# Softplus ahead of the residual and the logits, the first expert table in the last token tile, results ahead of ids, and own buffers for the last two results

## What is computed

```python
xs, z = split(x @ W_in.T)                       # 512 + 512
xc = silu(causal_conv_4_taps(xs) + conv_b)
a  = softplus((xc @ W_x.T)[:, :32] @ W_dt.T + b_dt)
x1 = layernorm(2 * x + (xc * a * silu(z)) @ W_out.T)
scores = sigmoid(x1 @ gate_w.T)                  # 16 experts in 4 groups of 4
# keep the 2 groups with the best sum of their 2 best (scores + bias); of these the top 4
# experts; weights = scores / their sum * 2.5
y = sum over the 4 experts of weight * (silu(x1 @ Wg) * (x1 @ Wu)) @ Wd   # inner size 128
y += (silu(x1 @ Ws_g.T) * (x1 @ Ws_u.T)) @ Ws_d.T                          # shared, 256
out = layernorm(2 * x1 + ... )                   # layernorm(x1 + (x1 + y))
```

## Time and profile before

| | |
|---|---|
| median of three runs | 603.64 us |
| profiled execution | 605.58 us, its span 603.8 us, mean granted TensorE clock 0.954 |
| TensorE busy / weight loads | 533.4 us (88%) / 449.9 us |
| VectorE | 434.6 us (72%) |
| ScalarE | 376.2 us (62%) |
| GpSimd | 335.4 us (56%) |
| chain that ended last | TensorE 55%, VectorE 24%, issue 7%, DMA 5% |

### The profile page before, as it was taken

How to read it: one execution, slowest core, us unless ns; L and a number is a source line. 1 busy time by engine, 2 the same in 40 slices (tenths; PEclk the granted TensorE clock), 3 DMA queues, 4 the chain that set the end, 5 groups by cost and what they waited for, 6 DMA issues and landing times.

```text
span 603.8 us, 11596 instructions
## 1 busy us (share of the span) xinstructions
PE 533.4 (88%) x3064; PEld 449.9 (75%) x3064; DVE 434.6 (72%) x1101; ACT 376.2 (62%) x960; POOL 335.4 (56%) x368
## 2 busy tenths in 40 slices
PE   2868899898998989979978899999999989998593
PEld 2557585676866768658666798999999979987582
DVE  3869689989899898997886567435344468787575
ACT  3675857757485574844813575777777847776452
POOL 2051112366666566645677657777777656667620
PEclk9989799999998999979989999999999979999797
DMA  8991402233232332311886647976666498973994
GB/s 190 288 276 58 149 36 105 86 120 128 78 131 83 114 119 80 119 41 69 278 319 227 215 151 235 316 249 220 204 196 208 163 351 268 298 247 107 389 316 140
DMA packets 70149, 111.19 MB, mean 184 GB/s; under 512 B 12644, under 2 KB 52965, under 8 KB 69576
## 3 DMA queue, kind: packets, MB, share of 16 engines
q1 hardware_dynamic: 52304, 71.11, 37.6%
q0 software_dynamic: 13056, 35.68, 16.1%
q10 hardware_dynamic: 4728, 3.67, 1.9%
HBM read 61.77 MB, written 50.74 MB: 186 GB/s over the span
## 4 chain that ended last, share of the span: by engine, by line
PE 55%; DVE 24%; issue 7%; DMA 5%; SPq 4%; ACT 3%; POOL 1%; ACTq 0%; DVEq 0%; POOLq 0%
PE psum L711 9%; PE psum L650 5%; PE psum L652 5%; PE psum L651 5%; PE psum L877 4%; PE psum L878 4%; PE psum L879 4%; PE psum L859 4%; DVE xc L1283 3%; PE psum L972 3%; PE psum L901 3%; PE psum L902 2%; PE psum L903 2%; PE psum L887 2%; SPq L507 2%
## 5 line engine op out<-in xcount | busy, mean ns | idle before, releaser
L601 POOL DMA_INDIRECT x_buf<-row,row_id x128 | 133.2, 1040 | 44.1 <-issue 35.3
L642 POOL DMA_INDIRECT y_buf<-y_out,y_ids x104 | 105.3, 1013 | 55.2 <-issue 28.5
L593 POOL TENSOR_TENSOR m<-xc,zs 128x512 f32<-128x512 f32 x32 | 42.7, 1355 | 119.2 <-DVE shift L1345 56.9
L1640 DVE TENSOR_TENSOR t_lo<-psum,t_hi 128x512 fp32r<-128x512 f32 x72 | 48.8, 685 | 55.8 <-ACT t_hi L1139 55.8
L877 PE MATMUL psum<-ew_gu_hi,t_hi 128*128 x288 | 85.8, 298 | 1.7 <-DVE t_lo L1640 1.0
L878 PE MATMUL psum<-ew_gu_lo,t_hi 128*128 x288 | 82.6, 287 | 0.0
L879 PE MATMUL psum<-ew_gu_hi,t_lo 128*128 x288 | 82.4, 286 | 0.0
L1283 DVE SCALAR_TENSOR_TENSOR xc<-psum,cw_taps,xc 128x511 f32<-128x511 f32 (+2 forms) x96 | 71.7, 747 | 8.2 <-ACT halo_x L996 5.5
L650 PE MATMUL psum<-x_hi,win_hi 128*128 128x512 f32 x128 | 54.9, 429 | 14.0 <-DVE win_lo L1605 10.7
L711 PE MATMUL psum<-wout,m 128*128 128x256 f32 x256 | 58.3, 387 | 3.9 <-DVE m L1309 3.9
L877 PEld LDWEIGHTS psum<-ew_gu_hi,t_hi 128*128 128x128 f32 x288 | 55.9, 194 | 4.2 <-issue 3.9
(11 more groups left out here) (231 smaller groups left out, 1339.1 us busy)
## 6 DMA issues: line engine op xcount, KB each, us to landing
tiles_in<-x_buf SPq DMA_DIRECT2D x144, 144.0 KB
y_in<-y_buf SPq DMA_DIRECT2D x32, 512.0 KB, 6.0
xT<-in_x_T SPq DMA_DIRECT2D x8, 512.0 KB, 3.8
xtok<-in_x_tok SPq DMA_DIRECT2D x8, 512.0 KB, 3.5
gu_hi_buf<-w_hi_now SPq DMA_DIRECT2D x8, 512.0 KB, 2.6
out_dram<-res ACTq DMA_DIRECT2D x7, 512.0 KB, 3.8
x_buf<-pad_row SPq DMA_DIRECT2D x17, 144.0 KB
raw_gu<-in_wg_T SPq DMA_DIRECT2D x16, 128.0 KB, 3.8
```

Source lines behind the costliest of these rows:

```text
L601: nc.gpsimd.indirect_dma_start(out=x_buf, out_offset=bass.IndirectOffsetOnAxis(ap=row_id[t % ROWS][:, b, k:k + 1], axis=0), in_=row[t % RO ...
L642: nc.gpsimd.indirect_dma_start(out=y_buf, out_offset=bass.IndirectOffsetOnAxis(ap=y_ids[:, q % IDS, i:i + 1], axis=0), in_=y_sent[:, i, :] ...
```

## The change

1. VectorE, tiles 1 to 6: softplus(t, 0) and its product come first, then the whole residual of t-2 (no longer split over two tiles), then the gate logits. For t > 2 the weight piece of the tile before stands between the two norm halves of tile t. TensorE has the ranks behind the dt matmuls instead of ahead of them. ScalarE's second silu of z goes behind a part of the convolution input.
2. The first table is made in tile 7, first of all on VectorE, and copied out behind the logits. TensorE runs ranks, shared up, table_mm(0), and then the output projection by pairs of channel groups, so that its first half needs only softplus(7, 0). The transposes of quad 0 follow undivided. The shared product follows the norm.
3. Quads: ScalarE makes result ahead of result_rows; TensorE states the waits for a_l and y_evac ahead of the second half of turn_x; in the last quad turn_act comes earlier and VectorE's act_low follows at once.
4. The results of the last two quads get buffers of their own, in tiles_in, and don't wait for a buffer.
5. Stores: blocks are stored in the groups of STORED_AT, and the last group as two.

```diff
         y_out += y_in[0:2]
+        y_out += [tiles_in[:, b, :, 0:D] for b in range(2)]
...
+        STORED_AT = {3: ((0, 4),), 7: ((4, 8),), 19: ((8, 12), (12, 16), (16, 20)), 23: ((20, 24),),
+                     25: ((24, 26),), 27: ((26, 28),)}
...
         def out_slot(j, u):
+            if u >= NQ - 2:
+                return RING + u - (NQ - 2)
             return u % RING if half_of(j, u) == 0 else u % 2
...
         def out_free(eng, j, u):
+            if u >= NQ - 2:
+                return
...
-            g = 2 * HG - 1
-            at_least(sp_, "o_done_dve", SUB)
-            sp_.dma_start(out.rearrange("(n p) d -> p n d", p=P)[:, SUB * g:SUB * (g + 1), :],
-                          res[:, SUB * g:SUB * (g + 1), :]).then_inc(s["stored"], 16)
+            for i in range(0, SUB, 2):
+                b = ACT_NORMED + i
+                at_least(sp_, "o_done_dve", i + 2)
+                sp_.dma_start(out.rearrange("(n p) d -> p n d", p=P)[:, b:b + 2, :],
+                              res[:, b:b + 2, :]).then_inc(s["stored"], 16)
...
+            def out_proj_by_pairs(t):
+                for i in range(PAIRS):
+                    at_least(pe, "y_done", PAIRS * t + i + 1)
+                    for b in range(SUB):
+                        o = psum[:, 4 + b // 2, (b % 2) * D:(b % 2 + 1) * D]
+                        for c in (2 * i, 2 * i + 1):
+                            mm = pe.matmul(o, m[:, c, b * P:(b + 1) * P], wout[:, c, :], start=c == 0 and b % 2 == 0,
+                                           stop=c == KI - 1 and b % 2 == 1)
+                        if b % 2 and i == PAIRS - 1:
+                            mm.then_inc(s["wout_mm"], 1)
...
-                if t > 1:
-                    ranks(t - 2, t)
                 if first:
                     z_proj(t + 1, 0)
                 dt_out(t, range(2, KI))
-                if t == TABLE_TILE + 1:
-                    table_mm(0)
+                if t > 1:
+                    ranks(t - 2, t)
...
+                    experts = tile_experts(q - 1)
+                    if q + 1 == NQ:
+                        turn_act(j, u)
+                    at_least(pe, "a_l", q)
+                    at_least(pe, "y_evac", q - 1)
                     if q + 2 < NQ:
                         turn_x(j, u + 2, range(1, KD))
-                    down(j, u - 1, tile_experts(q - 1))
+                    down(j, u - 1, experts)
...
-                    turn_act(j, u)
+                    if q + 1 < NQ:
+                        turn_act(j, u)
...
             gate_turn(t - 1)
+            ranks(t - 2, t)
             shared_up(t - 1, 0)
-            ranks(t - 2, t)
+            table_mm(0)
+            out_proj_by_pairs(t)
             at_least(pe, "table_done", 2)
-            turn_x(0, 0, range(0, 1))
-            out_proj(t)
-            turn_x(0, 0, range(1, KD))
+            turn_x(0, 0)
...
-                silu_z(t + 1, range(0, 2))
+                silu_z(t + 1, range(0, 1))
                 if not first:
                     shared_silu(t - 1, 0)
                 conv_in(t + 1, range(2, 3))
+                silu_z(t + 1, range(1, 2))
...
+            def store(first, end):
+                at_least(act, "o_done", end)
+                act.dma_start(out.rearrange("(n p) d -> p n d", p=P)[:, first:end, :],
+                              res[:, first:end, :]).then_inc(s["stored"], 16)
...
+                    if q > DEEP:
+                        result(j, u - 2)
                     if q == DEEP:
                         result_rows(j, u)
                     if q + 1 < NQ:
                         result_rows(j, u + 1)
-                    if q > DEEP:
-                        result(j, u - 2)
...
             def tile(t, first=False, more=True):
+                softplus(t, 0)
                 if t > 1:
-                    residual(t - 2, range(1, 2))
+                    residual(t - 2)
                 if not first:
                     gate_logits(t - 1)
-                softplus(t, 0)
-                if t == TABLE_TILE + 1:
-                    table_out(0)
...
-                norm_in(t, range(2))
+                norm_in(t, range(0, 1))
+                if t > 2:
+                    for i in PIECES_OF[t - 1]:
+                        weights_low(i)
+                norm_in(t, range(1, 2))
...
-                if t >= 2:
-                    for i in PIECES_OF[t]:
-                        weights_low(i)
-                if t == TABLE_TILE:
-                    first_table()
-                if not first:
-                    residual(t - 1, range(0, 1))
...
+                    if q + 1 == NQ:
+                        act_low(j, u)
...
             t = NT - 1
-            residual(t - 2, range(1, 2))
+            first_table()
+            softplus(t, 0)
+            residual(t - 2)
             gate_logits(t - 1)
-            softplus(t, 0)
+            table_out(0)
+            softplus(t, 1)
             place(t - 2)
-            softplus(t, 1)
             route(t - 1)
...
             norm_in(t, range(1, 2))
+            layer_norm(t)
             shared_act(t - 1, 1)
-            layer_norm(t)
```

32 lines of the change are left out of this document (15 added, 17 removed).

## The result

The changed kernel takes 606.59 us (median of 6 runs, 605.3 to 608.6) against 602.99 us for the kernel before in the same comparison: a ratio of 1.0062, 95% interval 1.0043 to 1.0081. It is slower by 0.6%, 3.6 us. Forecast were 601.2 us, faster; the time lies at the far end of the range (606.8), on the other side of no change. The profiled span is 606.8 us, against 603.8.

A forecast was written before the change was run, and what follows sets the result against it. Token tiles bound by a chain through VectorE and TensorE, neither alone; quads by TensorE, the end by waits on buffers and sums. Terms sum to -4.35 us from the profiled 605.58, giving 601.2 us, range 596.5 to 606.8.

The forecast's parts named there:

- Tiles 3 to 5: Middle token tiles, softplus first: 36.7 us a tile against 37.6, 0.9 less each, together -2.8 us (bounds -4.4 and -0.7).
- tile 6: Token tile losing the first table's operations and copies: from 40.7 to 36.7 us, -4.0 us (bounds -4.6 and -3.3).
- Tile 2: Ranks wait for product, whole residual and logits: shared up +0.95 us later, half clock likely at 1.3; sum +2.25 us.
- tile 1: Later logits delay ScalarE's exponential and the second softplus, so VectorE reaches the norm later: +0.9 us (bounds 0 and 1.0).
- The last tile: Late first table: VectorE stands before its copy, norm and shared down come later, transposes +7.2 us (bounds +3 and +9.6).
- The quads: Expert quads: result first gives -1.5 us in steady quads; -1.0 from quad 26 on; nothing up to quad 12.
- The end: After the last gate product: own buffers and earlier sums and sends give -4.7 us, stores by two blocks -0.7.
- part 4 of the theory: Theory after the two traces: the end is bound by GpSimd's sends and the last rows' landing, not by the buffers.
- rival 4: Tail gives little: sends, not buffers, set the last rows, +2.4 us; quads' gain lost, +1.0: 604.6 us; chance 0.13.
- Rival 3: Half clock everywhere: tiles 3 to 6 at 37.4 us, last tile's shared up and down at half: 606.8 us; chance 0.20.

The follow-up runs named there:

- kernel 4: Kernel before with only the changed quads and end (order of waits, own buffers, stores), all token tiles as before: 596.37 us, ratio 0.9898 to the kernel before.
- experiment 1: Changed kernel plus six idle matmuls ahead of the ranks in tiles 2 to 6: 0.990 of the kernel before (second run); tiles 3 to 6 36.54 to 36.78 us.
- kernel 3: Changed kernel with the first table in tiles 5 and 6 and the last tile's order as before: 601.0 us, ratio 0.9963 to the kernel before.
- experiments 7 and 8: Kernel 4 without own result buffers (last group 0.988), and kernel 4 with ScalarE's ids and weights ahead of result (0.976, 0.983, 0.978); all runs disturbed.
- kernels 3, 4 and 5: The fifth: changed kernel with z_proj ahead of the ranks and a new order of the last tile; 599.61 us, ratio 0.9946 to the kernel before.

## Why the prediction was wrong, point by point

**Tiles 3 to 5 (forecast -2.8, measured -0.2) and tile 6 (-4.0, -3.1).** This is the first step that failed: the cost of TensorE's half clock in a tile. The start of shared up was forecast at +22.0 us and came at +21.8; VectorE's arrival wasn't the limit. TensorE at half clock was put at +37.2 us, and I took 36.7, a value between full and half clock. A middle is a mean over tiles, of which about half would have had to stay at full clock; the stop of 1.8 us is in every tile, and every one of tiles 3 to 6 had the half clock and took 37.54 us, 0.34 more than even the half clock had been put at. The rows to go by were those of the same length: 1.74 us in two stops had brought the half clock in each of tiles 3 to 5 of the trace of before. In kernel 4 the old order had one tile at full clock too, with 36.11 us, so there was even less to gain than the trace of before showed: the 0.9 us forecast for the new order was nearly all clock, and at one and the same clock the order had little or nothing to give (experiment 1). What had spoken for the middle, tile 2 at full clock, was a stretch whose stops were differently placed, and after the change it too fell to 0.96. Experiment 1 shows the term: 0.9 us a tile with the stop filled. The five tiles 2 to 6 have 4.3 us in it.

**Tile 2 (+2.25, +2.64) and tile 1 (+0.9, +0.7)** came as worked out, the one with the half clock that was called likely. Of tile 1's part the order doesn't decide alone: kernel 3, with the same order, had 35.11 us there, with one stretch of half clock in it (mean 0.95) instead of two (0.90).

**The last tile (+7.2, +9.76)** was right in its mechanism, step for step: VectorE through logits at 302.6 (forecast 302.75), stop before the table (6.27, forecast 5), norm end 326.0 (325.2), shared down at 326.70 (325.9), stop of some 6 us (6.02). Mis-sized was what the half clock costs behind stops of 5 to 6 us. I let half of shared down's 16 matmuls return to full rate and got 5.2 us up to the transposes; it took 6.5, at half clock almost to its end. Here the half clock lasted not 3.5 us but 10.2, from 322.5 to 332.7, the last 6.0 of them with matmuls. Shared up behind the first stop had no full-rate matmul either (half clock from 302.0 to 308.8), so that the table was copied 28.8 us behind the norm half of tile 6 instead of the 27.7 forecast. These 1.3 and 1.1 us are nearly all of the 2.6. The kernel before had shown as much: behind its stop of 5.52 us at 567.01 the half clock went on to 571.8. The upper bound of 9.6 had this case, and 9.76 lies at it. With the gain in tile 6 the late table and its order are a loss of 6.6 us, as kernel 3 shows from the other side (a ratio of 0.996 instead of 1.006, 6 us).

**The quads (-2.5, -3.4).** The sum is near by luck, for its parts are not where they were put. Up to quad 12, where I took nothing, the first gate products gain 1.4 us (84.6 us from quad 0 to 12, now 83.2); from quad 12 to 26 it is 1.0 instead of 1.5, and from quad 26 on 0.9 instead of 1.0. Ten steady quads, 11 to 20, went from 58.58 to 58.02 us, 0.6; the 59.15 us of the earlier trace rows are 0.57 more than ten quads, so that the slack was 0.21 us a quad and not the 0.27 that I worked out. In these the result now ends at 454.25, 1.2 us ahead of the down projection's first load at 455.44, so that the wait of 0.24 us is gone; but the load then stands directly behind the transposes, which come later than I had thought, for the period is 5.8, not 5.7 us. In kernel 4 the three parts are 0.6, 2.1 and 1.3 us. Which of the edits gives them is open (experiments 7 and 8).

**The end (-5.4, -3.2).** The own buffers do what was said: no result waits for a buffer, and the last down projection stands 2.47 us instead of 5.52. But what is late next was taken wrongly. GpSimd's timeline of the end, the four sends of quad 35, and VectorE's, the last pair of rows:

```profile
577.83 0.99 POOL L653 DMA_INDIRECT y_buf<-tiles_in,y_ids  x1 [0.30 <-issue]
579.12 1.23 POOL L653 DMA_INDIRECT y_buf<-tiles_in,y_ids  x1 [0.30 <-issue]
580.65 1.06 POOL L653 DMA_INDIRECT y_buf<-tiles_in,y_ids  x1 [0.30 <-issue]
582.02 1.09 POOL L653 DMA_INDIRECT y_buf<-tiles_in,y_ids  x1 [0.30 <-issue]
594.66 0.69 DVE L1787 TENSOR_TENSOR y_in<-y_in 128x512 f32<-128x512 f32 x1 [0.92 <-DMA y_in<-y_buf]
```

The result of quad 35 was ready at 573.0, and its sends start at 577.83: they wait for their turn in GpSimd's queue, where the last 18 sends follow each other with 0.30 us between them (the 28 of three expectations is my miscount). From the last gate product to the end of the last send it took 26.1 us before and 25.0 after, 1.1 less, and the last pair of rows can be added 36.5 us after the last gate product, against 36.6 before. I had their sends start 1.6 to 2.5 us earlier and the rows land with them. Of the 1.1 us that came, 1.0 went again between the last send and the last pair (11.6 us instead of 10.6), and what takes it isn't shown. In kernels 3, 4 and 5, too, the last pair starts 36.45 to 36.6 us after the last gate product, whatever stands ahead. So the sums, which did start 4.6 us earlier against the last gate product (13.1 us behind it instead of 17.7), end no earlier than the rows allow: 1.6 us behind the last pair instead of 4.0. This is 2.4; from the sums' end to the end of the span lie 9.8 us instead of 10.5, the 0.7 of the stores. With the 0.1 of the last pair they are the 3.2. So part 4 of the theory is read from the rows of five traces and not shown by an experiment: the one on the buffers settled nothing. It is rival 4 in its first half ("if the last rows don't land earlier, because the sends and not the buffers set them"), at a price near the 2.4 us that it was given.

**Sum and rivals.** The sign of every term was right. The span moved by +3.0 us where -4.35 was forecast; the 7.3 between them are 2.6 in tiles 3 to 5, 0.9 in tile 6, 2.6 in the last tile, 0.4 in tile 2 and 2.2 at the end, less 0.9 in the quads, 0.2 in tile 1 and 0.2 ahead of it. Some 4.8 of these hang on the clock, 3.5 in tiles 3 to 6 and 1.3 in shared down. Rival 3, half clock everywhere, is what happened in the token tiles: 53.18 us from the norm half of tile 6 to the transposes (its point was 53), a stretch of half clock in each of tiles 3 to 6. That its 606.8 us and the median of 606.6 are so near is luck: it was summed from the profiled 605.58 us, and the profiled execution of the changed kernel took 608.60, 1.8 more, because the end gained less than the sum had it. It had a chance of 0.20, less than half of the forecast's. The trace had tiles 3 to 6 for it, and one row, tile 2, against.

## What to carry to other kernels

The granted clock has two levels, so a tile has two times, here about 37.6 and 36.1 us, and a cost half way between them is right only if as many tiles will be at the one as at the other. Count the tiles of the trace at either level behind stops of the same length (before the change all three of tiles 3 to 5 were at half, after it 14 of 15) and sum with the level that most of them have. Compare two orders at one and the same level, or the clock's gain is taken for the order's. Before merging two short stops into one long one, look for work of the same engine, here one projection, that can stand in the gap. And where an engine's queue holds a copy of another engine's result, count what stands behind the copy, then ask which loads the moved result releases: its price can hide behind the first loss and appear only when that is mended.

## What the runs showed that was not expected

- Idle matmuls made a tile shorter: 36.65 us instead of the 37.62 of the same group, with 1.4 us more of work in it.
- Half clock lasted much longer in the last tile than the 3.5 us of the middle ones: behind the stops of 5.8 and 6.0 us it stood from 302.0 to 308.8 and from 322.5 to 332.7.
- Softplus first, forecast at +0.35 us for tiles 1 to 5, costs 4.6 us by itself (kernels 3 and 4, some 1.4 of it the clock of one tile), and the kernel without it and without the late table is the fastest, with 596.4 us.
- The old order of a tile has two times, 36.1 and 37.6 us, in one and the same execution, by whether the clock stays up behind two stops of under 1 us each.
